# The step of phase 1 in a block-attention, convolution and mixture-of-experts kernel: turned rows in two PSUM banks, softmax halves back to back on VectorE, and another order of ScalarE's copies

## What is computed

```python
# attention / convolution part, per chunk of 64 positions
Xh = rfft(chunks, axis=2)                        # 33 frequencies
X_low, X_high = Xh[:, :, :4], Xh[:, :, 4:]
A_r, A_i = attention(X_low.real), attention(X_low.imag)   # 16 heads, 4 kv heads, block-causal softmax
H_r, H_i = causal_conv(X_high.real), causal_conv(X_high.imag)   # 7 taps per channel, gelu, 128x128
g = sigmoid(chunks.mean(axis=2) @ gate_w.T)
A_high = complex(H_r * g, H_i * g) + X_high
Y = irfft(concat([alpha * A_low + (1 - alpha) * X_low, A_high]))
x = layernorm(x + Y)
# experts: distances to 8 centroids, the two largest, softmax weights, two experts per row
d2 = |x|^2 + |centroid|^2 - 2 x @ centroid.T
x = layernorm(x + sum_e w_e * (silu(x @ Wg + bg) * (x @ W1 + b1)) @ W2 + b2)
```

## Time and profile before

| | us |
|---|---|
| median of 3 runs (577.01 to 577.7) | 577.16 |
| the profiled execution | 573.48 |
| its span, first to last instruction | 570.9 |
| TensorE busy in the span | 504.0 |
| VectorE busy | 364.7 |
| ScalarE busy | 349.9 |
| POOL busy | 289.6 |
| mean granted TensorE clock | 0.947 of full speed |

### The profile page before, as it was taken

One profiled execution on the slowest core, in us unless ns is written; L12 is line 12 of the kernel. 1 busy time (PEld: TensorE's weight loads), 2 busy tenths in 40 slices (PEclk: granted clock), 3 DMA queues, 4 the chain that ended last, 5 costly groups with the idle time before them and its releaser, 6 DMA issues.

```text
span 570.9 us, 13381 instructions
## 1 busy us (share of the span) xinstructions
PE 504.0 (88%) x3905; PEld 478.2 (84%) x3905; DVE 364.7 (64%) x1045; ACT 349.9 (61%) x743; POOL 289.6 (51%) x422
## 2 busy tenths in 40 slices
PE   5687998998998754789999999999999999999990
PEld 4585887887887643679999999999999999999980
DVE  4767888888888878623343456464646556666663
ACT  3564878878878544255555556657575666756551
POOL 0232464454454434254445445776777777654453
PEclk9978999999999955889999999999999999999995
DMA  9350344344442112010000000111111111100000
GB/s 220 121 135 13 94 120 123 98 123 123 96 124 75 40 42 18 10 26 22 17 21 16 21 21 21 35 35 40 31 39 34 36 34 35 38 20 16 20 29 28
DMA packets 47182, 31.54 MB, mean 55 GB/s; under 512 B 12123, under 2 KB 44710, under 8 KB 47126
## 3 DMA queue, kind: packets, MB, share of 16 engines
q1 hardware_dynamic: 42214, 21.77, 14.7%
q0 software_dynamic: 4096, 8.66, 5.7%
q10 hardware_dynamic: 816, 0.41, 0.3%
HBM read 22.13 MB, written 8.69 MB: 54 GB/s over the span
## 4 chain that ended last, share of the span: by engine, by line
PE 56%; DVE 4%; issue 1%; ACT 1%; DMA 0%; POOL 0%; DVEq 0%; ACTq 0%; POOLq 0%
PE ps L1594 26%; PE ps L1619 18%; PE ps L1609 9%; PE ps L1603 1%; PE ps L1452 1%; DMA xs<-rows_dram,idx 0%; DVE lohot L1282 0%; POOL out_dram L1555 0%; PE ps L1466 0%; PE ps L1431 0%; DVE hieq L1281 0%; DVE xs L1788 0%; ACT xs L1666 0%; DVE R L1252 0%; ACT L1694 0%
## 5 line engine op out<-in xcount | busy, mean ns | idle before, releaser
L1594 PE MATMUL ps<-wts,xh 128*128 x620 | 154.2, 332 | 1.3 <-ACT xh L1683 1.3
L1777 DVE TENSOR_TENSOR h<-ps,sg 128x684 f32<-128x684 f32 x78 | 67.6, 866 | 90.5 <-PE ps L1594 78.9
L1572 POOL TENSOR_TENSOR xl<-xT,xh 127x128 fp32r<-127x128 f32 x155 | 68.2, 459 | 96.9 <-ACT xh L1683 93.1
L1619 PE MATMUL ps<-w2s,hT 115*128 (+1 forms) x930 | 116.5, 274 | 0.3 <-DVE xs L1788 0.3
L1619 PEld LDWEIGHTS ps<-w2s,hT 115*128 115x128 f32 (+1 forms) x930 | 109.9, 191 | 0.6 <-issue 0.6
L1594 PEld LDWEIGHTS ps<-wts,xh 128*128 128x128 f32 x620 | 104.5, 190 | 1.5 <-issue 1.5
L1594 PE MATMUL ps<-wts,xl 128*128 x310 | 99.6, 321 | 0.0
L1694 ACT ACTIVATE sg<-ps 128x684 f32<-128x684 f32 x78 | 57.6, 739 | 66.2 <-PE ps L1594 66.2
L1703 ACT ACTIVATE hT<-ps 114x768 f32<-114x768 f32 x78 | 62.9, 807 | 55.8 <-PE ps L1609 55.8
L1788 DVE SCALAR_TENSOR_TENSOR xs<-ps,xs 128x128 f32 x155 | 54.4, 351 | 52.0 <-PE ps L1619 36.3
L1555 POOL DMA_INDIRECT out_dram<-xs,idx x64 | 63.0, 985 | 26.2 <-issue 17.5
(11 more groups left out here) (283 smaller groups left out, 843.1 us busy)
## 6 DMA issues: line engine op xcount, KB each, us to landing
xt<-_attn_hidden_states_dram SPq DMA_DIRECT2D x8, 512.0 KB, 6.2
xres<-_attn_hidden_states_dram SPq DMA_DIRECT2D x7, 512.0 KB, 5.3
rows_dram<-x1s SPq DMA_DIRECT2D x7, 512.0 KB, 3.7
w2s<-in_L_ffn_W_dram SPq DMA_DIRECT2D x8, 171.0 KB
st<-in_L_ffn_Wg_dram SPq DMA_DIRECT2D x8, 171.0 KB, 2.4
st<-in_L_ffn_W_dram SPq DMA_DIRECT2D x8, 171.0 KB, 2.4
stl<-in_L_ffn_Wg_dram SPq DMA_DIRECT2D x8, 171.0 KB, 3.2
stl<-in_L_ffn_W_dram SPq DMA_DIRECT2D x8, 171.0 KB, 4.0
```

Of the source, the lines that this page charges most:

```text
L1572: v.tensor_tensor(xl[0:D - 1, i % 2, u, :], xT[0:D - 1, bass.ds(off[u], P)], xh[0:D - 1, i % 2, u, :].bitcast(F32), ALU.subtract).then_inc ...
L1594: mm = pe.matmul(ps[:, 2 * w + u, 0:HF], a[:, t % 2, u, :], wflat[:, bass.ds(w1[u] + (b + w * HF), HF)], start=(k == 0), stop=(k == 2))
L1619: mm = pe.matmul(ps[:, low(t) + u, 0:D], hT[0:n, t % 2, u, k, :], w2flat[0:n, bass.ds(w1[2 + u] + k * D, D)], start=(k == 0), stop=(k == 2))
L1777: v.tensor_tensor(h[:, t % 2, 0:units(t), :], ps[:, 2:2 + units(t), 0:HF], sg[:, 0:units(t), :], ALU.mult).then_inc(s["h_done"], 1)
```

## The change

It touches only `step` of phase 1. The second group of turned rows goes through bank 0 and no longer waits for the first copy; ScalarE copies it from there; the products with cT wait for each half of x1T when they come to it. ScalarE's order becomes exponential 0, Vs 0, exponential 1, Vs 1, x1T 0, x1T 1. On VectorE taps 2 and 3 move from between the softmax instructions to behind the second reciprocal, and tap 4 to behind the residual. The numbers and sizes of the instructions stay as they are.

```diff
--- before.py
+++ after.py
@@ -436,9 +436,8 @@
             def step(t, X, Y, T):
                 def turned(h):
 
-                    pe.wait_ge(s["x1t_ev"], 2 * (t - 2) + h)
                     for j in range(4):
-                        mm = pe.transpose(ps[:, 7, j * P:(j + 1) * P], x1s[:, 4 * h + j, :], ident)
+                        mm = pe.transpose(ps[:, (7, 0)[h], j * P:(j + 1) * P], x1s[:, 4 * h + j, :], ident)
                     mm.then_inc(s["t_done"], 1)
 
                 if Y and not T:
@@ -536,6 +535,7 @@
                             mm = pe.transpose(ps[:, 2 + h, j * P:(j + 1) * P], VT[:, 4 * h + j, :, :].rearrange("p i f -> p (i f)"), ident)
                         mm.then_inc(s["vt_done"], 1)
                 if T:
+
                     turned(1)
                 if X:
 
@@ -550,8 +550,9 @@
 
                     if Y and X and isinstance(t, int):
                         pe.wait_ge(s["ct_zero"], 1)
-                    pe.wait_ge(s["x1t_ev"], 2 * (t - 1))
                     for j in range(TB):
+                        if j % 4 == 0:
+                            pe.wait_ge(s["x1t_ev"], 2 * (t - 2) + j // 4 + 1)
                         mm = pe.matmul(ps[:, 7, j * C:(j + 1) * C], x1T[:, j, :], cT[:, :], start=True, stop=True)
                     mm.then_inc(s["r_done"], 1)
 
@@ -664,7 +665,7 @@
 
                     act.wait_ge(s["t_done"], 2 * (t - 2) + h + 1)
                     act.wait_ge(s["r_done"], t - 2)
-                    nc.scalar.activation(x1T[:, 4 * h:4 * h + 4, :].rearrange("p j m -> p (j m)"), ps[:, 7, :], ACT.Copy).then_inc(s["x1t_ev"], 1)
+                    nc.scalar.activation(x1T[:, 4 * h:4 * h + 4, :].rearrange("p j m -> p (j m)"), ps[:, (7, 0)[h], :], ACT.Copy).then_inc(s["x1t_ev"], 1)
 
                 def gelu(b, i, first):
 
@@ -728,21 +729,17 @@
                     act.wait_ge(s["sub_done"], 2 * t + i + 1)
                     nc.scalar.activation(Sb[:, i, :, :], Sb[:, i, :, :], ACT.Exp, scale=1.0 / 8).then_inc(s["exp_done"], 1)
 
-                if X:
-                    softmax(0)
-                if T:
-                    turned(0)
-                if Y:
-
-                    for h in range(2):
+                for h in range(2):
+                    if X:
+                        softmax(h)
+                    if Y:
                         act.wait_ge(s["vt_done"], 2 * (t - 1) + h + 1)
                         if T:
                             act.wait_ge(s["z_done"], 2 * (t - 1))
                         nc.scalar.activation(Vs[:, 4 * h:4 * h + 4, :].rearrange("p j d -> p (j d)"), ps[:, 2 + h, :], ACT.Copy).then_inc(s["vs_ev"], 1)
                 if T:
+                    turned(0)
                     turned(1)
-                if X:
-                    softmax(1)
                 if X:
                     gelu(t, 0, not Y)
                 if X:
@@ -913,9 +910,7 @@
                     settle()
                 if X:
                     scores(0)
-                    conv(t, 1, not Y, range(2, 3))
                     scores(1)
-                    conv(t, 1, not Y, range(3, 4))
                 if X:
 
                     for i in range(2):
@@ -923,8 +918,7 @@
                         v.tensor_reduce(sm[:, i, :], Sb[:, i, :, :], AX, ALU.add).then_inc(s["sum_done"], 1)
                         dve.wait_ge(s["sum_done"], 2 * t + i + 1)
                         v.reciprocal(rs[:, i, :], sm[:, i, :]).then_inc(s["rec_done"], 1)
-                        if i == 0:
-                            conv(t, 1, not Y, range(4, 5))
+                    conv(t, 1, not Y, range(2, 4))
                 if Y:
 
                     dve.wait_ge(s["xres_in"], 16 * t)
@@ -935,7 +929,7 @@
                         xr = xres[:, 4 * h:4 * h + 4, :].rearrange("p j d -> p (j d)")
                         v.scalar_tensor_tensor(out=xr, in0=xr, scalar=2.0, in1=ps[:, 2 + h, :], op0=ALU.mult, op1=ALU.add).then_inc(s["zs_done"], 1)
                 if X:
-                    conv(t, 1, not Y, range(5, KS))
+                    conv(t, 1, not Y, range(4, KS))
                 if Y:
 
                     for j in range(TB):
```

## The result

The change makes the kernel **slower**: 582.16 us (median of 20 runs) beside 577.14 for the kernel before, a ratio of 1.0084 with a 95% interval of 1.0065 to 1.0102, where 574.1 was forecast. The profiled execution took 579.96 us, its span is 577.3.

The account below looks back on a forecast made before the run. The prediction took a chain through several engines and VectorE's residual to bound phase 1's step: 6 x 0.45 = 2.7 us plus 0.38 at t = 1, together 3.1 off 577.16, gives 574.1 us, range 571.0 to 576.7.

Parts of the forecast that it names:

- What bounds the step: Phase 1's loop: a chain through several engines and VectorE's residual sets the 21.45 us step; TensorE's L441 wait is off it.
- VectorE's stretch: First maximum to residual on VectorE: shrinks from 6.03 to 5.53 us, 0.50 a step.
- the first step: Phase 1's first step, without a residual: between +0.3 and -0.4 us, taken as nothing.
- The overlap: VectorE: an instruction not needing the one in front starts 0.08 or 0.09 us before its end.
- ScalarE in time: ScalarE's new order delivers in time; a late wait inside L555 costs 0 to 0.19 us; step gain taken as 0.45.
- What else moves: Other engines in the step: Pb starts 1.10 us earlier, gaining nothing; table load hidden by 0.1; taps 4 to 6 end later.
- VectorE's slack before XL: VectorE's idle time before XL falls from 0.74 to 0.16 us, so VectorE is not yet the bound.
- the sign the prediction named: Prediction is wrong if VectorE's wait before XL vanishes while the step stays long; a step of 21.0 us was expected.
- TensorE as the bound: Phase 1's loop: exponential 1 or L555's wait comes late, a step gains only 0.2 us; 575.8 us, chance 0.18.
- The clock that falls in the loop: TensorE's clock drops to 0.50 at L453 and L417, costing 1.66 us a step; 579.1 to 584.0 us, chance 0.07.
- The clock that stays up at t = 1: TensorE's idle time at t = 1 shortens to about 1.7 us, saving another 1.66; 572.4 us, chance 0.12.
- From the loop to the kernel: Summing over steps: six at 0.45 us give 2.7, t = 1 gives 0.38, the first step nothing; together 3.1.

Follow-up runs that it names:

- the last two versions: Versions of the change with its banks and ScalarE's exponential 1 behind Vs 1: taps 3 and 4, or taps 2 to 4, behind the residual; 574.04 and 577.09 us.
- the bank edit alone: Kernel before with only the second transposes through bank 0 without the wait, products with cT waiting half by half; 577.14 us, ratio 1.0013.
- Pb cut: Changed kernel with POOL's Pb product cut to 8 elements per partition instead of 512, the rest a constant; 574.24 us, ratio 0.9947.
- the version with two PSUM inputs: Changed kernel, but from t = 1 taps 2 and 3 each take their first input from PSUM instead of SBUF; 574.78 us, ratio 0.9969.
- one PSUM input: Changed kernel, but from t = 1 tap 2 alone reads PSUM and tap 3 keeps two SBUF inputs; 576.79 us, one run.
- taps 3 and 4 late: Changed kernel with tap 2 back between the softmax instructions, taps 3 and 4 behind the residual, ScalarE's Vs 1 before exponential 1; 574.04 us, ratio 0.9948.
- taps 2, 3 and 4 late: Changed kernel with taps 2 to 6 all behind the residual and ScalarE's Vs 1 before exponential 1; 577.09 us, ratio 1.0006.
- ScalarE's order and banks: Changed kernel with VectorE's old order put back, keeping ScalarE's new order and the route through bank 0; 577.80 us, ratio 1.0002.
- tap 4 alone late: Changed kernel with taps 2 and 3 back between the softmax instructions, tap 4 behind the residual, ScalarE's Vs 1 before exponential 1; 575.33 us, ratio 0.9973.
- VectorE's order alone: Kernel before with only VectorE's new order of taps, keeping ScalarE's old order and bank 7; 595.22 us, ratio 1.0315.

## Why the prediction was wrong, point by point

*What bounds the step.* Right: the chain through the residual sets it. In every kernel but the last two versions, and but for the steps with a fallen clock, the step moved with the residual's place (6.03 gives 21.45, 6.39 gives 21.80, 7.45 gives 22.85, 5.49 gives 20.90), and the bank edit alone, which takes away TensorE's largest wait, gave nothing.

*VectorE's stretch.* This is the step that failed, in one term: "A tap right behind a tap needs its result: 0.64 + 0.03 = 0.67", and with it the tap behind the reciprocal at its old duration. The durations were read from taps that run while POOL is idle or has not yet begun to read. The prediction moved Pb 1.10 earlier and the taps later and never laid the one over the other; it looked at POOL's queue ("nothing gains") but not at what POOL and VectorE share, so the collision was a term put at nothing without a reason. The two taps cost 2.19 instead of 1.30: 0.50 of gain became 0.36 of loss a step. VectorE's other terms came out within 0.04: with the collision removed the stretch is 5.49. A second term was mis-sized for the same reason: the first step was "taken as nothing" and came out 1.60 longer, though only a part of that is the collision's, as the next paragraphs show. The overlap that the prediction set against a sentence of the Trainium skill (VectorE: DVE Perf Modes, "The DRAIN you can't avoid") held: the second reciprocal, reached by those distances, came within 0.04 of its place. But the same section goes on to say that a next instruction which nothing holds starts earlier, so page and rows don't contradict each other there.

The rows of before held the hint. The last two taps of the first step, 1.83 us under Pb, were called unusual and set down as noise of 0.3 to 0.4 either way; they are the same collision (Pb runs from 27.23 to 29.84 there, and takes 2.61 for two). The first step pays it again: with five taps behind each other VectorE's timeline of the changed kernel shows

```profile
27.07 4.10 DVE L832 SCALAR_TENSOR_TENSOR YI<-XF,dw,YI 128x416 f32<-128x416 f32 x5
```

where five undisturbed taps take 3.19 (Pb cut) to 3.23. Their end holds the spectrum copy, and XL starts 9.76 after the first maximum instead of 9.12. The half-speed stretch of TensorE's clock there lasted 10.2 instead of 6.8 us (0.51 from 28.4 to 38.6 in the view by stretch; 0.50 from 29.0 to 35.8 before). The collision doesn't explain that: the version with two PSUM inputs has the same first step, with 4.11 for the five taps, but a stretch of 6.8 and 23.14 us for the step; the one with one PSUM input has 10.2 and 24.56; before, the step took 22.75, in the change 24.35. So of the 1.60 some 0.4 come with the new order and its collision, and the rest with the longer stretch, whose cause stays open.

The Trainium skill states the rule (SBUF — State Buffer, "SBUF: two separate sides"): VectorE with two SBUF inputs, against a GpSimd instruction that reads SBUF, takes a shared pair of ports as an exclusive lock for the whole instruction, and the other fully blocks. The runs agree with it: 0.86, 1.39 and 1.30 with the collision, 1.18 for tap 3 alone in it, about 0.65 a tap without (1.30 for two). It was the rule that spoke against this change, and I weighed two others.

*ScalarE in time.* Right: exponential 1, Vs 1 and L556 came within 0.25 us of their places and bind nothing at 21.80.

*What else moves.* Pb starts 1.1 earlier relative to the step, as said. VectorE's slack before XL, forecast 0.16, is 0.06 (the statistics end at 125.36, the spectrum copy at 125.42), because the taps end 0.9 later than forecast. That is the sign the prediction named, a vanished wait beside a long step; still the wait before XL isn't what makes the step long, as the spectrum copy sets XL's start and TensorE goes from L462 to the projections without idle time.

*The rivals.* TensorE as the bound: not in the change (it idles 1.00 at L452); at 20.90, in the version with two PSUM inputs, the products with cT end at 117.70 and the residual at 117.67, so both bind together. The clock that falls in the loop: see above. The clock that stays up at t = 1: not in the change, whose TensorE idled 2.66 there instead of the forecast 1.7 and whose clock fell again (0.52 from 55.7 to 59.1). It did stay up with one PSUM input (2.31 idle), with taps 3 and 4 late (1.66) and with taps 2, 3 and 4 late (1.19); from the first maximum of t = 1 to that of t = 2 these took 21.38, 20.43 and 20.82 us, the kernel before 22.87. The rival on the slower side had the wrong mechanism for this change and so too small a chance.

*From the loop to the kernel.* In the profiles, first maxima of before and after stand 0.32 apart at t = 0 and 4.31 apart at t = 7: 1.60 from the first step, 0.48 and 0.48 from the next two, 0.35 to 0.37 from each of the others. So from t = 1 to t = 7 the change lost 2.39, where the prediction had it gain about 2.6. Phase 2 starts 5.04 later (213.46 against 208.42). That this is the difference of the medians (5.02) is luck: the 0.32 ahead of t = 0 is small beside the 4.1 by which the first maxima of all the kernels' profiles differ (22.17 to 26.31), and the profiled spans differ by 6.4. The other 1.4 lies in phase 2, where TensorE's clock had a half-speed stretch of 10.2 us instead of 3.4 soon after the experts begin. Phase 2 lasts 362.5 to 364.4 us in the profiles: 362.5 in the three with one such stretch of 3.4 (before, banks alone, ScalarE's order and banks), 363.8 and more in those with 6.8 or more. This is a part of why tap 4 alone late saves 2.93 from t = 0 to t = 7 and its median shows only 1.5 (575.33 beside 576.86); what decides where the stretches fall was not tried and stays open.

## What to carry to other kernels

Before an instruction is moved, lay it over the other engines' timelines at its new place and ask what they share, not only who waits for whom: here a VectorE instruction with two inputs in SBUF and a POOL instruction that reads SBUF never moved data at the same time, while one of VectorE's with a PSUM input did. An outlier in the duration of an instruction of fixed size (1.25 for 0.59) can have a neighbour that explains it; look for the neighbour before calling it unusual. Work placed between dependent instructions may stand where it does because nothing collides there. And when a transfer begins to bind, follow what issues it: here it hung, over three engines, on the very instructions that had been moved.

## What the runs showed of the hardware that I had not expected

POOL's half of the collision is as exact as VectorE's: Pb takes 1.04 us alone and 1.39 when a tap holds it up. In the kernel before, one tap started 0.17 ahead of Pb and came through in 0.60, and Pb then took longer (2.39 for two instead of 2.04): the one that begins first wins, so a shift of 0.2 us decides who pays.

TensorE's clock fell to 1.2 GHz in a loop whose longest idle time of TensorE was 1.77 us (VectorE's order alone), and not in one with 1.00 and 0.76 (the change) or 1.33 and 0.36 (before). Idle time alone doesn't sort the cases: at t = 1 the clock fell after 2.21 us (tap 4 alone late) and stayed up after 2.31 (one PSUM input).
